# A fused attention and expert layer: an accumulation moved ahead of a subtraction, a routing scan spread over four units, and one score tile cut as 384 and 256 columns

## The reference

```python
q, k = rope(q), rope(k)
attn = softmax(where(causal, -inf, einsum('bihd,bjhd->bhij', q, k) * scale))
o = einsum('bhij,bjhd->bihd', attn, v)
out = x + (o @ wo.T + bo + residual) + moe(xn) + shared(xn)
# routing: slot of a token = running count of its expert's picks
pos = (cumsum(one_hot(expert), axis=0) * one_hot(expert)).sum(-1) - 1
```

## Time and profile before

| | us |
|---|---|
| median of three runs | 1061.93 |
| lowest and highest | 1060.56 and 1063.89 |
| the profiled execution | 1061.38 |
| its span, first to last instruction | 1059.5 |
| PE busy | 1022.0 (96%) |
| DVE, ACT, POOL busy | 726.5, 659.0, 749.8 |

### The profile page before, as it was taken

The page is one execution under the profiler, slowest core; times in us unless marked ns, Lnnn a source line. Parts: engine busy times, 40 slices in busy tenths (PEclk is TensorE's granted clock), DMA queues, the critical chain, the costliest instruction groups (busy, mean ns, idle before and its releaser), DMA issues.

```text
span 1059.5 us, 18814 instructions
## 1 busy us (share of the span) xinstructions
PE 1022.0 (96%) x6500; PEld 915.8 (86%) x6500; DVE 726.5 (69%) x1747; ACT 659.0 (62%) x1450; POOL 749.8 (71%) x654
## 2 busy tenths in 40 slices
PE   3999999999998999999999999999999999999997
PEld 3898888888887888888998989998988989999896
DVE  6867778877789766766666666666666666665667
ACT  4566665656665666666665666756576665666663
POOL 4825776777676575787778697877878778787770
PEclk9999999999999999999999999999999999999999
DMA  7211326212221221323232323323223322231232
GB/s 237 61 57 40 93 67 124 65 27 46 50 61 36 40 46 41 64 69 83 53 97 71 79 69 88 98 46 80 71 74 95 84 73 63 66 80 29 43 100 80
DMA packets 51629, 75.42 MB, mean 71 GB/s; under 512 B 12240, under 2 KB 29008, under 8 KB 51408
## 3 DMA queue, kind: packets, MB, share of 16 engines
q1 hardware_dynamic: 46144, 67.66, 24.1%
q0 software_dynamic: 5392, 6.56, 3.9%
HBM read 33.94 MB, written 10.90 MB: 42 GB/s over the span
## 4 chain that ended last, share of the span: by engine, by line
PE 81%; DVE 6%; POOL 6%; ACT 3%; DMA 2%; issue 1%; SPq 0%; DVEq 0%; POOLq 0%; ACTq 0%
PE ps L294 23%; PE ps L296 22%; PE ps L295 22%; PE ps L417 9%; PE ps L500 2%; DMA qs<-qb 2%; POOL qb L1586 1%; POOL qb L1582 1%; POOL qs L1583 1%; DVE ps L1435 1%; PE ps L512 1%; DVE acc L1475 1%; POOL q_l L1115 1%; ACT prob L994 1%; PE ps L326 0%
## 5 line engine op out<-in xcount | busy, mean ns | idle before, releaser
L1582 POOL TENSOR_TENSOR qb<-qb,k_sb 128x512 f32<-128x512 f32 x128 | 170.3, 1331 | 221.6 <-DMA qs<-qb 221.0
L1435 DVE CUSTOM_DVE_ANT_0 ps<-ps,maskr 128x128 f32<-128x128 f32 (+7 forms) x256 | 193.7, 763 | 56.7 <-PE ps L296 56.3
L994 ACT ACTIVATE prob<-ps,nmax 128x128 f32<-128x128 f32 (+7 forms) x256 | 190.3, 743 | 62.6 <-DVE nmax L1435 60.8
L1005 ACT ACTIVATE ptd_h<-ps 128x128 fp32r<-128x128 f32 (+3 forms) x256 | 108.6, 436 | 171.9 <-PE ps L417 170.9
L1586 POOL TENSOR_TENSOR qb<-qb,qs 128x512 f32<-128x512 f32 x128 | 165.6, 1294 | 19.0 <-POOL qs L1583 1.0
L1445 DVE TENSOR_TENSOR ptd_l<-ps,ptd_h 128x128 fp32r<-128x128 f32 (+3 forms) x256 | 124.6, 487 | 79.1 <-ACT ptd_h L1005 75.3
L417 PE MATMUL ps<-k_sb,prob 128*128 128x128 f32 x1152 | 171.9, 273 | 2.1 <-ACT prob L994 1.0
L1583 POOL TENSOR_TENSOR qs<-qs,k_sb 128x512 f32<-128x512 f32 x128 | 171.7, 1341 | 0.0
L417 PEld LDWEIGHTS ps<-k_sb,prob 128*128 128x128 f32 x1152 | 135.6, 141 | 18.3 <-issue 2.7
L294 PE MATMUL ps<-k_h,q_h 128*128 128x512 f32 (+3 forms) x384 | 141.1, 367 | 3.3 <-ACT prob L994 2.4
L296 PE MATMUL ps<-k_h,q_l 128*128 128x512 f32 (+3 forms) x384 | 132.9, 346 | 0.0
(11 more groups left out here) (178 smaller groups left out, 2613.4 us busy)
## 6 DMA issues: line engine op xcount, KB each, us to landing
qs<-qb SPq DMA_DIRECT2D x256, 128.0 KB
ew<-epack SPq DMA_DIRECT2D x16, 768.0 KB, 4.3
rqk<-wqk SPq DMA_DIRECT2D x16, 256.0 KB, 2.9
xt<-x SPq DMA_DIRECT2D x4, 512.0 KB, 4.7
rv<-wvp SPq DMA_DIRECT2D x8, 256.0 KB, 3.3
ro<-wop SPq DMA_DIRECT2D x16, 128.0 KB, 2.3
token_table<-xn SPq DMA_DIRECT2D x4, 512.0 KB, 4.8
token_sum<-token_table SPq DMA_DIRECT2D x1, 2048.0 KB, 9.4
```

The costliest lines, as they stand in the source:

```text
L994: act.activation(prob[:, t % 2, 0:w], score[t % 2][:, 0:w], ACT.Exp, bias=nmax[:, t:t + 1], scale=-1.0, accum_out=rsum[:, t:t + 1]).then_i ...
L1005: act.activation(turned(0, t, j0, w), src, ACT.Copy).then_inc(pth_done, 1)
L1435: dve.tensor_tensor_reduce(out=score[t % 2][:, 0:w], in0=score[t % 2][:, 0:w], in1=maskr[:, SEQ - w:SEQ], scale=-1.0, scalar=3e38, op0=ALU ...
L1582: pool.tensor_tensor(qb[:, i, :], qb[:, i, :], cos_sb[:, c], ALU.mult).then_inc(rope_a, 1)
```

## The change

Three edits. The DVE list has `add_out(n - 1, 1, 1)` ahead of `v_lo(n, 0)`. The fifth score tile (t = 4, 640 columns) lies 128 columns into its area, and is computed as 384 and 256 columns instead of 512 and 128, so that each piece stays inside a bank. The four blocks of turned marks stand at four places of unit 8 instead of two, and the scan, the two searches and the four small instructions move to `route(9, 0)`, `route(10, 0)`, `route(11, 0)` and `route(11, 1)`.

```diff
+        tile = [score[t % 2][:, P * (t == 4):P * (t == 4) + (t + 1) * P] for t in range(TILES)]
...
-                dst, i = score[t % 2], slice(t * P, (t + 1) * P)
+                dst, i = tile[t], slice(t * P, (t + 1) * P)
+                mid = CH - P * (t == 4)
                 for c in range(t // 4 + 1):
-                    w = min(CH, (t + 1) * P - c * CH)
-                    j = slice(c * CH, c * CH + w)
+                    j = slice(c * mid, min((t + 1) * P, mid + c * CH))
...
                 project(n + 1, 2)
+                masks(n, 2)
                 turn(n, 3)
...
                 scores(n, 6)
+                masks(n, 3)
                 outproj(n - 1, 1, 1)
...
-                elif k == 3 * MASKS + 1:
+                elif k == 3 * (MASKS + 1):
                     route_scan()
-                elif k == 3 * MASKS + 2:
+                elif k == 3 * (MASKS + 2):
                     route_find(0)
-                elif k == 3 * MASKS + 3:
+                elif k == 3 * (MASKS + 3):
                     route_find(1)
-                elif k == 3 * MASKS + 4:
+                elif k == 3 * (MASKS + 3) + 1:
                     route_take()
...
                 turned_lo(n, 4)
+                add_out(n - 1, 1, 1)
                 if n:
                     v_lo(dve, n, 0)
-                add_out(n - 1, 1, 1)
                 turned_lo(n, 5)
```

More of the change, by code:

```diff
@@ L520, in bias_row, with masks @@
                 pe.matmul(take("CB", 0)[:, 0:DM], ones[:, :], cacc[:, :], start=True, stop=True).then_inc(cbm_done, 1)
-            def masks(n, half):
+            def masks(n, q):
                 if n != MASKS:
                     return
-                if half == 0:
+                if q == 0:
                     pe.wait_ge(m4_ready, 2)
[L527 to L531, removed]
+                bank = take("MT", q).bitcast(BF16)
+                for i in range(GT):
+                    ins = pe.transpose(bank[:, i * P:(i + 1) * P], m4[:, q * GT + i, :], maskb[:, 0:P])
+                ins.then_inc(mtm_done, 1)
             pe.wait_ge(id_in, 16)
@@ L993, in exps @@
                 w = (t + 1) * P
-                act.activation(prob[:, t % 2, 0:w], score[t % 2][:, 0:w], ACT.Exp, bias=nmax[:, t:t + 1], scale=-1.0,
+                act.activation(prob[:, t % 2, 0:w], tile[t], ACT.Exp, bias=nmax[:, t:t + 1], scale=-1.0,
                                accum_out=rsum[:, t:t + 1]).then_inc(exp_done, 1)
@@ L1039, in bias_row, with masks @@
                 act.activation(cbc[:, :], rbank("CB", 0)[:, 0:DM], ACT.Copy).then_inc(cb_done, 1)
-            def masks(n, half):
+            def masks(n, q):
                 if n != MASKS:
                     return
[L1044 to L1047, removed]
+                act.wait_ge(mtm_done, q + 1)
+                act.activation(mt[:, q * CH:(q + 1) * CH], rbank("MT", q).bitcast(BF16)[:, 0:CH],
+                               ACT.Copy).then_inc(mt_ready, 1)
             for n in range(UNITS):
@@ L1434, in maxes @@
                 w = (t + 1) * P
-                dve.tensor_tensor_reduce(out=score[t % 2][:, 0:w], in0=score[t % 2][:, 0:w], in1=maskr[:, SEQ - w:SEQ],
+                dve.tensor_tensor_reduce(out=tile[t], in0=tile[t], in1=maskr[:, SEQ - w:SEQ],
                                          scale=-1.0, scalar=3e38, op0=ALU.add, op1=ALU.min,
```

## The result

The changed kernel takes **1049.47 us** (median of four runs, 1048.64 to 1049.79). The kernel before, run beside it, takes 1061.24 (four runs, 1059.61 to 1063.89). The ratio is 0.9887, with an interval from 0.9868 to 0.9907: faster by 1.1%. A later set of runs of the same changed kernel gave 1050.15 (ratio 0.9890, 0.9876 to 0.9904). The kinds of gain were forecast rightly, but their sum was 9.6 and came out as 11.8; another 0.7 lies in the kernel before, which had 1061.93 in its first runs and 1061.24 in these.

A forecast was written before the change was run, and what follows sets the result against it. PE was taken to bound the kernel, busy 96% of the span. Terms -4.6 (tile), -3.0 (addition), -3.0 (unit 8), +0.1 (marks), +0.9 (scan) sum to -9.6, predicting 1052.3 us, range 1050.2 to 1055.5.

The forecast's parts named there:

- What bounds it: Whole kernel: PE is busy 96% of the span, so gains come from PE's own stream or its waits.
- The score tile: Tile 4 in all 32 units: 384 and 256 columns save 0.145 us a unit, 4.6 in all.
- the check for slack: Behind tile 4, read in unit 9: the projection's bank has 1.3 us of slack against 0.145, so all 4.6 is kept.
- The addition: Ahead of the low part: PE's 0.74 us wait for `acc` goes in units 4, 6, 10, 12, not 2; gain 3.0.
- The router's last part, taken away: Unit 8: without the scan on DVE, PE's waits for the additions of the output projection go; gain 3.0 us.
- the 1.92 and 1.08: PE's two waits in unit 8 for late additions, the second containing the 0.74; both go without the scan, 3.0 us.
- The marks: Unit 8: PE passes some 0.5 us earlier and pays 0.6 two blocks later, a loss of 0.1.
- The scan, put in: Unit 9: the scan delays `ol`, so PE's projection waits 0.25 to 1.3 us; 0.9 was taken as the loss.
- The additions gave back: Rival, units 4, 6, 10, 12: another wait replaces the 0.74 as in unit 2; 1055.3 us, chance 0.09.
- the tile saved: Opposes the rival that 384 and 256 columns cost PE as much as 512 and 128; 1056.9 us, chance 0.05.
- POOL held nobody up: Opposes the rival that the scan holds POOL over 4.4 us, delaying ACT's first exponential of unit 10; 1055.3, chance 0.07.
- ACT and DVE read the new tile as before: Opposes the slower rival: DVE and ACT read tile 4 more slowly across two banks; about 1065 us, chance 0.02.

The follow-up runs named there:

- tile_only: The kernel before with only the fifth score tile cut as 384 and 256 columns: 1055.66 us, ratio 0.9955.
- wide0: The kernel before with score tile 0 computed over 256 columns instead of 128, the added half unused: 1062.33 us beside 1061.13, ratio 1.0009.
- wo_first: The kernel before with `cacc` and `wol` of unit 8 ahead of the scan on DVE instead of behind it: 1059.69 us, ratio 0.9986.
- scan_twice: The changed kernel with the scan of unit 9 done a second time behind the first: 1056.73 us in one run.
- the half scan: The changed kernel with router pieces and marks spread further and unit 9's scan in two halves, one beat apart: 1045.83 us, ratio 0.9863.

## Why the prediction fell short

Step by step, in its own order.

**What bounds it: right.** Nothing but PE's stream and PE's waits made the time.

**The score tile: right.** 4.6 was forecast; 4.7 stands in the traces of the changed kernel and of `tile_only`. (The 4.8 in the time of `tile_only` is no second proof, since its trace holds other steps of 1.7.) `wide0` shows the cause. Missed was unit 3, where PE gets to a bank sooner than DVE empties it and gives 0.32 back; the check for slack looked at one unit only.

**The addition: right mechanism, term too small.** Four units gained and unit 2 did not, as forecast, and the wait of 0.74 in unit 4 ended the way that the earlier trace rows suggested. DVE in unit 4 of the changed kernel:

```profile
211.78 0.69 DVE L1449 TENSOR_TENSOR ptr_l<-ps,ptr_h 128x512 fp32r<-128x512 f32 x1
212.38 0.87 DVE L1479 SCALAR_TENSOR_TENSOR acc<-ps,rinv,acc 128x256 f32<-128x256 f32 x2
213.54 0.69 DVE L1126 TENSOR_TENSOR v_l<-ps,v_h 128x512 fp32r<-128x512 f32 x1 [0.29 <-ACT v_h L816]
```

But "Four times 0.74: 3.0" took the idle time for the price, and that step failed. It was 4 x 0.98 = 3.9.

**The router's last part, taken away: right sum of causes, one cause misnamed, term too small.** "Without the scan both go" held, but 3.7 came back for the 1.92 and 1.08. Some 0.5 of the missing 0.7 is the same mistake as above (2.17 for 1.92, 1.35 for 1.08). Another 0.16 was gained at the turn between the two (337.52), for a reason not shown. And `wo_first` and `tile_only` show that the 1.92 goes too when the scan stays, once `cacc` doesn't meet POOL.

**The marks: wrong sign.** Forecast was a loss of 0.1, measured a gain of 0.3. The wait of 0.95 ahead of `weighted` is as forecast (0.9); the gains around it are 0.77 instead of 0.5, and the two later blocks cost some 0.5 instead of 0.6 (0.24 and 0.21 where they stand, the rest behind them). The forecast priced a block at 0.3; the one taken away gave 0.47 in one step. Why a block costs more at one place than at another was not followed further.

**The scan, put in: mechanism right, term too large.** Forecast was 0.9, bounds 0.25 and 1.3. The wait was 0.21 and cost 0.45, and unit 10 gave 0.21 back. DVE and POOL of the changed kernel in unit 9:

```profile
347.84 4.69 DVE L1365 TENSOR_TENSOR_SCAN rb_<-ra_,zcol 128x2048 f16<-128x2048 bf16 x1
...
353.52 0.66 DVE L1462 TENSOR_TENSOR ol<-ps,oh 128x512 fp32r<-128x512 f32 x1
...
355.44 1.16 DVE L1144 SCALAR_TENSOR_TENSOR cacc<-ro,bias,cacc 128x256 f32<-128x256 f32 x1
```

```profile
346.97 1.29 POOL L1586 TENSOR_TENSOR qb<-qb,k_sb 128x512 f32<-128x512 f32 x1 [4.13 <-DMA qs<-qb]
348.21 5.42 POOL L1587 TENSOR_TENSOR qs<-qs,k_sb 128x512 f32<-128x512 f32 x1
...
355.01 1.30 POOL L1119 TENSOR_TENSOR k_l<-qb,k_h 128x512 fp32r<-128x512 f32 x1
...
358.21 1.29 POOL L1586 TENSOR_TENSOR qb<-qb,k_sb 128x512 f32<-128x512 f32 x1 [1.90 <-DMA qs<-qb]
```

What failed here is "I take 0.9, nearer to the row of `cacc`". By starts, as the forecast reckoned this term, its 0.25 and the 0.27 below would have been 0.52, near the 0.45. POOL's instruction was not just begun when the scan came; it had 0.42 left (347.84 to 348.26), and the scan grew by 0.27, from 4.42 to 4.69. The next POOL instruction was then held to 5.42, and POOL made it up out of its idle time, of which 1.90 was left ahead of 358.21, as the forecast had it.

The Trainium skill (SBUF — State Buffer, section Who interferes with whom) says that a DVE instruction with two SBUF inputs contends with a GpSimd one that reads SBUF. By that rule, the trace agrees in both directions, 0.27 on DVE and 4.1 on POOL.

**The rivals.** None of the four came. The additions gave back only in unit 2, the tile saved, POOL held nobody up even in `scan_twice`, and ACT and DVE read the new tile as before (0.80 and 0.82 on average, in both kernels).

**In sum.** Of the 2.2 by which the gain was larger than forecast, the waits' true price is 1.6 (0.9 in the additions, 0.7 in unit 8, of which 0.2 is unexplained), the marks 0.4, the scan 0.65, the tile 0.1; 0.3 goes off for unit 3. That is 2.4, within what the runs tell. So the main step that failed is the price of a vanished wait: its idle time was taken for all of it (3.0 and 3.0), where the starts gave 3.9 and 3.7. The second is the scan in unit 9, put at 0.9, which cost 0.24 net. The remaining 0.7 below the forecast is the first runs of the kernel before. The range allowed for each cost of unknown size, but a wait that was read from the trace had no bound of its own.

## What to carry to other kernels

The idle time that a trace puts beside a matmul starts at the modelled end of the one before, and matmuls that don't wait start ahead of that end. So a wait that vanishes is worth its idle time and that overlap, 0.24 us here behind a turn, while one that grows or shrinks is worth just the difference. Price a wait by starts: how far apart the two instructions start with it, and how far apart the same two start where there is none.

When an instruction takes three times its usual duration, look for what another engine did at its start before blaming what stands ahead of it: an exchange of two calls gave here what moving 4.4 us of work gave.

When a kernel with a single edit gains, look in its trace at which places the gain arose. `tile_only` gained 2.0 us at a wait that its edit most likely had nothing to do with.

## What the runs showed of the hardware

- **How long DVE is held beside POOL.** The extra time of a DVE instruction with two SBUF inputs was a little less (0.14 to 0.20) than what POOL's running instruction had left: 1.26 left, 1.07 more (`cacc` before); 0.87 left, 0.68 more (`cacc` at 355.44, beside POOL's from 355.01); 0.42 left, 0.27 more (the scan). POOL in turn was held by nearly what DVE's instruction had left: 4.32 left, 4.13 more (5.42 instead of 1.29, beside the scan); 2.19 left, 1.99 more (3.28, beside the half scan). Not every POOL instruction does this: beside its indirect transfer `token_sum`, with 0.96 left at 811.15 of the changed kernel, `cacc` took its usual 0.48.
- **A long wait can cost more than itself.** Behind an idle time of 4.92 PE's clock was at its lower level for some 6 us, which cost 2.6 on top (one run). Of three traces with a wait of 1.92 to 1.97 in unit 8, one had a lower stretch of 3.4 behind it and two had none.
- **Dips without a wait.** The clock fell for some 3.4 us at a time between 30 and 87 us in several profiles, at different places, and not at all in others. The one at 58 us put PE 1.5 behind, of which 0.6 lasted. A page's slice reads 9 with one such dip in it, and 8 with the two of `wide0` (32.4 and 39.2).
